# A one-core recurrent block: first sequence's combine, gate and statistics one attention step earlier, gather in contiguous rows

## What is computed

```
xn = layernorm(x)
x  = x + attn0(xn) * silu(moe(xn))          # causal attention, 2 heads; 8 experts, top 2
xn = layernorm(x)
x  = x + attn1(xn) * silu(tanh(chain(xn)))  # rmsnorm, conv, decayed scan, memory, gated feed-forward
```

## Time and profile before

| | |
|---|---|
| median of 3 runs | 540.2 us (539.59 to 540.52) |
| the profiled execution's own time | 540.95 us |
| its span, first to last instruction | 538.8 us |
| PE / DVE / ACT / POOL busy | 519.0 / 397.5 / 314.6 / 223.7 us |
| granted TensorE clock | 1.00 over the whole span |

### The profile page before, as it was taken

The page is one execution under the profiler, slowest core; times in us unless marked ns, Lnnn a source line. Parts: engine busy times, 40 slices in busy tenths (PEclk is TensorE's granted clock), DMA queues, the critical chain, the costliest instruction groups (busy, mean ns, idle before and its releaser), DMA issues. The chain is left out here.

```text
span 538.8 us, 12865 instructions
## 1 busy us (share of the span) xinstructions
PE 519.0 (96%) x3195; PEld 387.7 (72%) x3196; DVE 397.5 (74%) x1129; ACT 314.6 (58%) x832; POOL 223.7 (42%) x229
## 2 busy tenths in 40 slices
PE   9998898999998999999999999998999999999997
PEld 4755566666667999999999999986454545544544
DVE  6889669768885766777677767766788887788654
ACT  4733554555547656666666666667776576657512
POOL 4304453666640333333333333332667557623310
PEclk9999999999999999999999999999999999999999
DMA  9930743311126555555555555618300000000001
GB/s 283 395 115 28 229 152 127 99 60 66 40 45 52 155 131 156 132 155 138 152 137 152 141 151 141 151 47 225 94 0 21 0 20 21 19 0 21 19 7 33
DMA packets 84722, 55.37 MB, mean 103 GB/s; under 512 B 52928, under 2 KB 69600, under 8 KB 84432
## 3 DMA queue, kind: packets, MB, share of 16 engines
q1 hardware_dynamic: 80368, 46.04, 32.7%
q0 software_dynamic: 4320, 8.92, 4.6%
HBM read 37.62 MB, written 15.74 MB: 99 GB/s over the span
## 5 line engine op out<-in xcount | busy, mean ns | idle before, releaser
L1808 ACT ACTIVATE AR<-bank,BGT 128x128 f32<-128x128 f32 x284 | 81.2, 368 | 71.8 <-PE bank L870 69.6
L580 POOL DMA_INDIRECT rows_y<-YO,W1E x71 | 68.8, 969 | 126.5 <-DVE YO L1335 123.9
L541 POOL DMA_INDIRECT slots_x<-XR,SLOT x64 | 62.5, 977 | 52.6 <-DMA slots_x<-XR,SLOT 32.7
L1358 DVE SCALAR_TENSOR_TENSOR AR<-bank,B1T,AR 128x128 f32<-128x128 f32 x284 | 80.2, 344 | 5.1 <-ACT AR L1808 3.6
L870 PE MATMUL bank<-AR,WGE 128*128 128x128 f32 x568 | 76.7, 278 | 1.9 <-DVE AR L1341 1.7
L888 PE MATMUL bank<-W2E,AR 128*128 x568 | 75.1, 275 | 0.5 <-DVE AR L1358 0.5
L879 PE MATMUL bank<-AR,WGE 128*128 128x128 f32 x568 | 75.0, 275 | 0.0
L1724 ACT ACTIVATE AR<-bank,AR 128x512 f32<-128x512 f32 (+1 forms) x64 | 33.8, 528 | 64.2 <-DVE AR L1268 53.4
L870 PEld LDWEIGHTS bank<-AR,WGE 128*128 128x128 f32 x568 | 69.0, 192 | 2.9 <-issue 2.5
L888 PEld LDWEIGHTS bank<-W2E,AR 128*128 128x128 f32 x568 | 69.1, 192 | 0.7 <-issue 0.7
L879 PEld LDWEIGHTS bank<-AR,WGE 128*128 128x128 f32 x568 | 69.1, 192 | 0.0
(11 more groups left out here) (214 smaller groups left out, 910.9 us busy)
## 6 DMA issues: line engine op xcount, KB each, us to landing
WGE<-in_wgu SPq DMA_DIRECT2D x71, 256.0 KB
XG<-slots_x SPq DMA_DIRECT2D x140, 32.0 KB
slots_x<-W1E SPq DMA_DIRECT2D x7, 585.0 KB, 10.1
X<-in_x SPq DMA_DIRECT2D x8, 256.0 KB, 5.1
SPARE<-in_wgu SPq DMA_DIRECT2D x1, 2048.0 KB
W2E<-in_w SPq DMA_DIRECT2D x1, 2048.0 KB
XR<-rows_y SPq DMA_DIRECT2D x8, 256.0 KB, 4.9
XNT<-rows_y SPq DMA_DIRECT2D x8, 256.0 KB, 5.4
```

What stands on the lines that cost most here:

```text
L541: pool.indirect_dma_start(out=slots_x, out_offset=bass.IndirectOffsetOnAxis(ap=SLOT[:, k, n:n + 1], axis=0), in_=XR[:, n, :], in_offset=No ...
L580: pool.indirect_dma_start(out=rows_y, out_offset=bass.IndirectOffsetOnAxis(ap=DST[:, j:j + 1], axis=0), in_=YO[q % 2][:], in_offset=None). ...
L1358: s = dve.scalar_tensor_tensor(out=HT[u][:, c, :], in0=B[3 + u][:, c * P:(c + 1) * P], scalar=B1T[:, bass.ds(e, 1), c], in1=ZB[u][:, c, :] ...
L1808: act.activation(ZB[u][:, c, :], B[1 + u][:, c * P:(c + 1) * P], ACT.Gelu, bias=BGT[:, bass.ds(e, 1), c]).then_inc(c_gelu, 1)
```

## The change

Four things are done.

- VectorE: `d_first_both` goes from step 4 to step 3, the product from 5 to 4, the gate and the sum from 6 to 5, the statistics from 7 to 6. The aggregate and the radicands move into step 7, where they stand at the same place of the list as before.
- GpSimd: `scales(0)` goes ahead of `both(2)`, and the wait on `d_x1` ahead of `both(2)` goes.
- ScalarE: `d_front2(2)` goes behind `d_turned(0)`. TensorE: `keep_warm(3, 8)` becomes `keep_warm(3, 3)`.
- `rows_y`: token `n*128 + p` now stands in row `p*32 + n` of each half, so that a partition's four rows of a transfer lie side by side: one run of 2 KB in place of four of 512 bytes. The tags that GpSimd scatters by change with it.

```diff
-        rows_y_t = rows_y[0:2 * TOKENS, :].rearrange("(k n p) d -> p k n d", k=2, p=P)
+        rows_y_t = rows_y[0:2 * TOKENS, :].rearrange("(k p n) d -> p k n d", k=2, p=P)
...
             both(1)
-            pool.wait_ge(d_x1, 1)
+            scales(0)
             both(2)
-            scales(0)
             front(1)
...
-            keep_warm(3, 8)
+            keep_warm(3, 3)
...
+                    if last and k == 3:
+                        d_first_both()
                     if last and k == 4:
-                        d_first_both()
+                        d_first_product()
                     if last and k == 5:
-                        d_first_product()
+                        d_first_gate()
                     if k in (5, 6):
                         combine(b, k - 5)
...
                     if last:
                         if k == 6:
-                            d_first_gate()
+                            d_stats(0)
                         if k == 7:
-                            d_stats(0)
+                            d_stats_settled(0)
+                            d_aggregate(0, MV0)
+                            d_radicands(0, MV0, VV0)
...
             attend(NB, NB % 2, first=True, last=True)
-            d_stats_settled(0)
-            d_aggregate(0, MV0)
-            d_radicands(0, MV0, VV0)
             d_early_gate(1)
...
             finish(NB)
-            d_front2(2)
             act.wait_ge(d_zero, 4)
             d_turned(0)
+            d_front2(2)
...
-    tags[:, :, :, 0] = TOKENS * np.arange(2)[None, :, None] + P * np.arange(NT)[None, None, :] + r[:, None, None]
+    tags[:, :, :, 0] = TOKENS * np.arange(2)[None, :, None] + np.arange(NT)[None, None, :] + NT * r[:, None, None]
```

## The result

The changed kernel takes 544.84 us (median of 12 runs), the kernel before 540.31 us (12 runs): 1.0091 times as long, 95% interval 1.0065 to 1.0118. It is slower by 4.5 us. The forecast was 2.7 slower (542.9), with a range to 544.6. The direction was right; the size was too small, and the result lies 0.2 us above the range. Of all the runs reported here one is left out of its ratio, a run of experiment 11 that took 1064.83 us, about twice as long as its others.

What follows compares the result with a forecast made beforehand. TensorE, always busy in the second block, bounds it, so a later start at the transposes shifts the end. +0.47 (step 6 held) + 0.4 (gather, first lock) - 0.21 (power wait) + 2.04 (two turns) = +2.7: 540.2 to 542.9 us, range 540.3 to 544.6.

Steps and rivals of the forecast that it cites:

- Gather and first lock: Seam: `d_first_both` waiting for the gather's landing, and `both(1)` holding the ports against the gate, together +0.4 us.
- the clock: Rival: TensorE's wait of some 3.2 us halves its clock for the first matmuls behind it, 545 to 547 us; chance 0.07.
- The two turns of GpSimd: Ahead of the HS1 transposes: `both(2)` and `front(1)` get in between VectorE's four tensor_scalar, +2.04 us.
- VectorE keeps its turn: Rival: VectorE runs all four tensor_scalar before GpSimd is served; +1.25 us, 541.4; chance 0.23.
- no exclusion: Rival: `both(2)` runs beside the four tensor_scalar without shutting them out; +0.65 us, 540.85; chance 0.10.
- Step 6 held: Attention: gate and sum ahead of step 6's maximum delay it 1.01 us, and the exponential of step 7 by 0.47.
- the wait on the power: Ahead of the transposes: the tensor_scalar no longer wait 0.21 us for GpSimd's power L607, -0.21 us.

Runs made afterwards that it cites:

- experiment 11: The kernel before with three warm-ups in place of eight ahead of the HS1 transposes, nothing else: 0.9992 times the kernel before.
- experiment 2: The changed kernel with GpSimd's old order (wait for the sum, `both(2)`, then `scales(0)` and `front(1)`): 1.0049 times the kernel before.
- experiment 3: As experiment 2, and `front(1)` waits until the four tensor_scalar are done: 1.0018 times the kernel before.
- experiment 4: The changed kernel with `combine(0)` ahead of the gate in step 5, all else as changed: 1.0114 times the kernel before.
- experiment 5: The changed kernel with eight warm-up matmuls ahead of `weigh` of step 4 and fifteen ahead of the transposes: 1.0042 times the kernel before.
- experiment 6: The changed kernel with GpSimd's `both(1)` held until the sum with X is done: 1.0033 times the kernel before.
- experiment 9: The changed kernel measured again without edits, on another chip: 1.0087 times the kernel before.
- Experiment 7: The kernel before with GpSimd's new order alone (`scales(0)` ahead of `both(2)`, no wait for the sum): 1.0002 times the kernel before.
- experiment 1: The kernel before with the new `rows_y` layout and matching tags alone: 1.0008 times the kernel before.
- experiment 8: The changed kernel with `combine(0)` ahead of the gate, both `both` behind the sum, `front(1)` behind the tensor_scalar, `keep_warm(3, 8)`: 0.9967 times the kernel before.
- experiment 12: The kernel before with the new `rows_y` layout, and `both(1)` held until VectorE's product is done: 1.0008 times the kernel before.
- Experiment 10: Split version of the changed kernel: `combine(0)` before gate, sum in step 6, statistics in step 7, long GpSimd operations held, six warm-ups: 0.9994 times the kernel before.

## Why the prediction was right in direction and short in size

Two terms of the sum failed. "Gather and first lock", taken as 0.4 us, measured 1.06. The clock, which had no term in the sum and 0.4 us in the range, cost 0.56 more in the traced seam and more than that over all runs; the rival "the clock" looked for it behind the transposes. The step that was left out is `combine(0)`, which TensorE waits for and which the change pushes down. The two turns of GpSimd, the greatest term, were right.

Each step, counted from the maximum of step 0 (the forecast's times, less 363.38, beside the trace's, less 364.94):

| | before | forecast | measured |
|---|---|---|---|
| gate asked for | | +8.52 | +8.63 |
| gate held by `both(1)` | | 0.2 | 0.99 |
| maximum of step 6 | +9.34 | +10.75 | +11.41 |
| exponential of step 7 | +12.08 | +12.95 | +13.89 |
| tensor_scalar asked for | +15.03 | +15.90 | +17.12 |
| the four tensor_scalar take | 1.12 | 3.16 | 3.02 |
| transposes of HS1 | +16.61 | +19.31 | +20.40 |

**The two turns of GpSimd: right.** Forecast +2.04, measured +1.90 (3.02 - 1.12). The places differ by one: I had GpSimd come in behind the first and the second tensor_scalar, and it came in ahead of the first, by 0.05 us, and behind it. By the Trainium skill (SBUF — State Buffer, SBUF: two separate sides) the port pair that VectorE and GpSimd share is held "for the whole instruction"; the trace agrees, and adds that the lock is given up between two instructions of a run: the second tensor_scalar took 1.30 us, though nothing but the first stood ahead of it on VectorE. Experiments 2 and 3 take the turns away one by one (2.09, 1.11 us). They are worth most: with what follows from them for the clock, the ratio goes from 1.0091 to 1.0018. By the rivals' test, whether the four take 1.12 us, "VectorE keeps its turn" and "no exclusion" have fallen.

**Why they could happen.** The forecast put the start of `both(2)` 0.06 us behind that of the tensor_scalar, a margin much smaller than the errors of its own terms; that it came out is in part luck. The runs show it to be steadier than that: in the five profiles with both halves of the change (the changed kernel, experiments 4, 5, 6 and 9) `both(2)` starts between 0.05 us ahead of the first tensor_scalar and 0.24 behind it, and the four take 3.02 to 3.19 us each time. Experiment 7 shows the other outcome. The four start early enough, `both(2)` is late, there are no turns, and nothing is lost that the time shows.

**The gather and the first lock: mis-sized.** The term was 0.4 (0.1 for the landing, 0.2 to 0.3 for the lock). The landing was right: `d_first_both` started at 370.99, which is 369.43 in before's time for the 369.3 that I took, and made the maximum behind it 0.15 late (371.60, +6.66, for +6.51 in experiment 11, whose order there is before's). The lock was not. I took 371.0 for `both(1)`, a guess between two bounds; it came at 373.43 - 364.94 = +8.49, or 371.87 in before's time. That is 0.14 ahead of the gate, close to the worst place, and cost 0.99 of the 1.0 that I had named as the bound. The maximum of step 6 is 0.66 later than forecast for it. How near the worst place it comes is in part chance: in the six profiles with the new layout and a gate in step 5 in which nothing holds `both(1)`, it starts between +8.05 and +9.31, and the gate takes 0.69 (experiment 4) to 1.76 us (experiment 5). That it starts sooner than before's +8.87 in most of them goes with SyncE's faster issues (experiment 1), a row which I had and did not read that way: eight issues of 0.5 to 1.0 us each over 11 us. From the fixed cost of about three cycles for each packet that the Trainium skill gives (DMA: Bandwidth & Descriptors, Why small descriptors are slow) the prediction estimated a landing some 0.2 us sooner with runs of 2 KB; no run here shows that, and what the runs show is the shorter issue.

**The overtaken `combine(0)`: missed, and it acts through the clock.** I had priced the maximum of step 6 (1.01 late, 0.47 at the exponential of step 7) and passed over `combine(0)`, which moves behind gate and sum with it. `weigh` of step 4 waits for it, and TensorE's list has the scores of step 7 behind `weigh`. In the changed kernel the exponential of step 7 was not set by ScalarE's order, as I wrote. It was released by the maximum of step 7, after a wait of 0.18 us, and that maximum by TensorE (0.38 idle, for L751). It makes +13.89, 0.94 later than forecast. 0.66 of that stand at the maximum of step 6 already and come from the gather and the lock. The other 0.28, and 0.28 more until the tensor_scalar are asked for (3.23 us for 2.95), came in while TensorE ran at half clock.

With the clock at 2.4 GHz the pushed-down `combine(0)` cost nothing by itself. From the maximum of step 6 to the first tensor_scalar the forecast had 5.15 us. It is 5.06 to 5.08 in experiments 2, 4, 5, 6 and 8, where the clock did not fall in between, with `combine(0)` ahead of the gate or behind it. It is 5.71 in the changed kernel and 6.08 in experiments 3 and 9, where the clock fell in between. So a fall there costs 0.65 to 1.02 us. These three are also the profiles in which `weigh` waited 1.97 to 1.99 us for `combine(0)`; with waits of 0.99 to 1.50 thereabouts (experiments 2, 4 and 6), or with warm-ups in it (5), none came there. That the wait brings the fall is argued from this, and from the mean clock of experiment 5.

**The clock: the rival that came true in part.** I gave it a chance of 0.07 and expected it behind the transposes. It fell in the seam in the profile shown, and in a second run (experiment 9) in both places. Seam and rest of that run are 20.95 + 160.48 = 181.43 us, against 178.76 in experiment 5, which has the same order and no fall. Over all runs the mean clock is about 0.005 under before's. One fall over 3.4 us at half speed lacks 1.7 us of full speed; 0.005 of 544 us is 2.7 us, or 1.6 falls more in each run than before has. Some of that lies in waits and costs nothing. Experiments 5 and 9 put what it costs at 2.4 us, 5 and the first measurement at 2.6, with the overlap of their intervals.

**The profile's 1.55 us ahead of the seam** are no effect of the change that any run shows. Two falls of the clock stand there (at 29.3 and 169.3), and before's profile had none, but runs of before have them on each chip (clock 0.995), and the profiles of experiments 9, 11 and 12 have two there as well. One of the falls of the changed kernel:

```profile
169.25:172.66 3.41, 3.41 (x18) 3.41 (x17) 0.12 (x1) 1.63 (x5) 0.00 (x0) 0.50 0.89 16
```

**The sum again.** Step 6 held 0.47 (the forecast's figure, not measured by itself), gather and first lock 1.06 (forecast 0.4), half clock 0.56 (forecast nothing), the wait on the power -0.21 as forecast: together the tensor_scalar start 1.88 later (forecast 0.66). With the turns, +1.90 (forecast 2.04), it is 3.79 in all in the seam, for 2.70. One sign of the forecast came out the other way: the power L607 starts at +14.67, 0.9 later than before and not 0.2 to 0.6 earlier, since it follows the late maximum of step 7. That changed nothing, as the tensor_scalar no longer wait for it. The measured 4.5 us lie above the profile's 3.8. Falls of the clock behind the transposes, of which this profile had none and that of experiment 9 had one, would account for this; no run shows how often they come. The upper end of the range, 4.4 us over before, held the lock at its bound (1.0) and 0.4 for a short fall; the second fall of experiment 9 alone made the rest 1.7 longer.

**What stays open.** How the loss divides between turns and clock is not additive: without the turns (experiment 3) the long wait ahead of the transposes goes too (1.02 us for 2.93), and perhaps with it falls behind them. And whether 0.9967 (experiment 8) is more than chance isn't settled; before and the split version could not be told apart.

## What to carry to other kernels

Work that is moved up on one engine pushes down what it overtakes. List that, and follow each item to who waits for it: here the thing overtaken was a 0.35 us `combine` that a matmul waited for. The wait, 1.97 us, would have cost nothing by itself, but the clock fell behind it. Where two engines shut each other out of SBUF, a queue of short instructions is the weak side: GpSimd's 1.25 us operations got in between 0.34 us ones, so hold the long operation with a semaphore until the short run is through (experiments 3 and 8). And a start that had slack only by when another engine's data happened to land is no constant: shift the data (a faster issue is enough) and the collision goes somewhere else, as to the product in experiment 1, to the gate in the changed kernel and to the sum in experiment 4.

## What the runs showed of the hardware

**A power on GpSimd does not shut VectorE out for its whole time; a product of 512 columns does.** Experiment 10, GpSimd and then VectorE:

```profile
375.00 1.00 POOL L608 TENSOR_TENSOR SPARE<-SPARE,HALF 128x4 f32<-128x4 f32 x1
```

```profile
375.04 1.12 DVE L1422 TENSOR_SCALAR SPARE<-X,SPARE 128x128 f32<-128x128 f32 x4 [0.21 <-POOL SPARE L607]
```

The power of four columns and the four tensor_scalar run side by side. The power takes 1.00 us, as the lone one of the first stage did (1.01), and the four 1.12, where they took 1.11 in experiment 8, where the power ended 0.2 us behind their start. In experiment 2 `front(1)`, beside the same four, stretched them to 2.09.

**The faster issue.** With a partition's rows side by side, SyncE takes 0.43 us for most transfers of 256 KB into Y1 (median 0.43 to 0.51, at most 0.73 in eleven profiles); with four runs 0.51 at least, 0.75 to 0.83 in the median and up to 1.10 (experiment 7's gather). The eight of Y1 start over 7.4 us (367.6 to 375.0) for 11.2.

**At the seam the clock fell from 2.4 to 1.2 GHz near waits of 2 us and more; elsewhere the waits do not tell.** TensorE's waits at the seam and the falls near it: 1.19 and 1.32 us (experiment 11), no fall; 1.29 (7) and 1.26 (12), none; under 1 us (1, 5, 8 and 10), none; 1.99 (3), a fall 0.2 us behind it; 1.98 (9), 0.4 us behind it; 1.97 (changed kernel), 0.9 us behind it; 1.21 and 2.00 (2), 0.99 and 2.96 (6), and 1.50 and 3.10 (4), a fall between 0.3 us ahead of and 1.1 us behind the transposes' start. A wait alone doesn't decide it: the 2.93 us of the changed kernel's profile, 1.5 us after one fall had ended, brought no second one, where 3.03 in experiment 9 did. Outside the seam it is plainer still. All fourteen profiles have a wait of 1.9 us that ends near 46 us and one of 1.65 to 1.8 that ends between 163.6 and 169.1 us; five of them show a fall within 1.3 us of the first, five within 1 us of the second, and before's shows none. The fall at 29.3 us of the changed kernel came with TensorE busy for the whole 3.3 us ahead of it. This is the fall of experiment 2:

```profile
378.43:381.84 3.41, 3.27 (x5) 1.49 (x5) 2.09 (x8) 2.49 (x6) 2.34 (x2) 0.50 0.03 7
```
